# Cross products by chunk halves, layer norm on VectorE alone, and a new order of all engines in a gated delta rule kernel

## Chip, core and metric

One core of one Trainium2 chip runs the whole program. The metric is the device time in microseconds (us) of one execution. Of the kernel before there are three timed runs, and one more under the profiler.

## What is computed

One transformer block on x of shape (4 sequences, 1024 tokens, 256), in float32. A vector c gives six modulation vectors per sequence; layer norm with scale and shift feeds a gated delta rule with 16 heads of 64, and a mixture of 8 experts (2 of them per token) follows. What matters here is the delta rule:

```python
q = silu(causal_conv(x @ Wq.T)); k = ...; v = ...      # 4 taps each
k = k / norm(k)
alpha = sigmoid(h @ Wa.T + ba); beta = sigmoid(h @ Wb.T + bb)
def step(S, xs):                                        # 1024 tokens, 16 heads, 4 sequences
    upd = vt - at * (S @ kt)
    S = clip(at * S + bt * outer(upd, kt), -5, 5)
    return S, S @ qt
y = scan(step) ; out = (y * silu(h @ Wg.T + bg)) @ Wo.T
```

## The kernel before, in words

**Parts.** `front` (L132) loads x, normalises it, forms the modulation, the transposed input `hT` and the decay factors. `delta_fast` (L457) holds the instruction streams of all five engines for the delta rule, with those of `front` woven in. `attn_out` and `moe` follow after a barrier; they are untouched. A slow path (`project`, `scan`) runs only if a bound on the state was exceeded.

**Turns.** The 16 heads and 4 sequences are worked off in 16 turns (`TURNS`): turn u has the head pair u // 2 and the sequence pair u % 2. A turn is 16 chunks (`NCW`) of 64 tokens, and a chunk is made of two blocks of 32 tokens. Within a chunk the delta rule needs the inverse of a unit triangular 64 x 64 matrix. GpSimd inverts the 32 x 32 diagonal blocks by substitution (`solve`, L952 and L957, 31 steps, for all chunks, heads and sequences at once). The lower left block comes from two more products on TensorE, 32 x 32 each:

- `cross_first(u, k)` (L1547, matmul L1556) multiplies the off-diagonal block by one inverse; `keep_cross_first` (ACT, L768, L771) copies the result from PSUM to SBUF.
- `cross_second(u, k)` (L1560, matmul L1566) multiplies by the other inverse; `keep_cross` (ACT, L774, L778) copies it, negated, into `XTz`, beside the diagonal blocks that `keep_x` (ACT, L760, L765) wrote there.

The argument k is the head of the pair. One call goes through its 16 chunks and, inside, the 2 sequences b2. Operands and results lie in 32-row quadrants of the partitions, given by `quad(b2, s)`; the rows of the result also depend on the head (`cross_at`): head 0 writes quadrant (b2, s), head 1 quadrant (b2, 1 - s). So one call writes two of the four quadrants, and its 32 matmuls alternate between them. Each float32 matmul of the program stands in the trace twice.

**A software pipeline written out by hand.** The loop `for it in range(1, TURNS + 2)` stands once for each engine. In iteration `it`, turn tc = it - 1 runs its chain of chunks, turn u = it is prepared (q and v projections, solve, cross products), turn un = it + 1 gets its k projection, and turn tb = it - 2 has its bound checked. Each engine works strictly in the order in which the code issues. Inside, `c` counts the chunks of the chain. One link of the chain is `seed_u` and `state_into_u` (PE), `keep_u` (ACT, L733), `state_sum` (PE, L1616), `state` (DVE, L1055). All other work is set between the links.

**Around the end of an iteration** the order before is: PE `cross_first(u,0)`, `state_sum(13)`, `cross_first(u,1)`, `seed_u(14)`, `state_into_u(14)`, `state_sum(14)`, `cross_second(u,0)`, `seed_u(15)`, `cross_second(u,1)`, `z_turned(tb,1)` (L1544), `state_into_u(15)`, `w_product(u,0)` (L1582), `seed_u(u,0)`, `y_of_u(tc,6)` (L1644), `kk(un,0)`, `kk(un,1)` (L1463), `proj_q(un,0,0)`. ACT: `keep_x`, `keep_cross`, `keep_u(15)`, `silu_k(un)` (L699), `keep_w` (L794), `join` (L751), `keep_u(0)`. DVE: `tap_k` (L1027), `decay` (L1102), `largest_k` (L1143), `bound_scan`, `bound_max`, `solve_matrix(un)` (L1114), `update_max`, `scale_v` (L1174), `turn_matrix` (L1122), `norms`, `scalars`, `state(0)`. `kk(un,0)` writes the PSUM banks that `w_product(u,0)` used and waits for `keep_w(u,0)`; `proj_q(un,0,0)` waits for `solve_matrix(un,0)`.

**The start.** In `front`, DVE takes the moments of all four sequences and normalises sequences 0 and 2 (L297), GpSimd sequences 1 and 3 (`normalise_pool`, L344). ACT makes each sequence's root (`root`, L232) between its other work; DVE inverts it (L292). PE turns the rows (`turned`, L375). The modulation matrix `wm` comes in one transfer of 1.5 MB before sequence 1, and all its columns' products are waited for (`s_v` 4) before rows 512 to 1023 are turned. Then follow the first turn's k path, `solve(0)`, and the decay factors, which pass through HBM: `turn_gammas` (L339), eight stores, `gamma_rows(0)`, `decayed_q(0)` (L1154).

## Time and profile before

| | us |
|---|---|
| median of three runs | 1978.79 (1976.9 to 1979.03) |
| the profiled execution | 1984.33 |
| its span, first to last instruction | 1982.8 |
| start, up to the first `keep_u` of turn 0 | 151.5 |
| from there to the first `keep_u` of turn 15, 15 intervals | 1088.8 |
| last turn's chain and the end of the delta rule | about 80 |
| gate, output projection and experts | about 663 |

Busy shares of the span: PE 85%, weight loads 60%, DVE 70%, ACT 45%, POOL 56%. An interval between two turns is 70.3 to 74.5 us, 72.6 in the mean. A turn is counted from its first `keep_u`, which is easy to find: it is the first L733 on ACT behind a `join` (L751). In the timeline a row is one run of equal instructions of one engine; what stands in square brackets is the idle time before it and what ended that.

### The profile page before, as it was taken

The numbers are of one execution on the slowest core, as the hardware profiler recorded it, in microseconds if no ns is written. First come the engines' busy times: TensorE is split into PE (matmuls) and PEld (weight loads), VectorE is DVE, ScalarE is ACT, GpSimd is POOL, SyncE is SP. The second block draws the span as 40 slices with busy tenths as digits, with TensorE's granted clock in tenths as the row PEclk, the third lists the DMA queues.
The fourth block names the chain that finished last, engine by engine and source line by source line (L and its number), as shares of the span: only waits on it lengthen the run. The fifth ranks groups of instructions, "written<-read, shape, count | busy, mean of one in ns | idle before, by whom it ended". The sixth has DMA issues, their size and how long they took to land. (4 is left out here: it accounts for less than half of the span.)

```text
span 1982.8 us, 59488 instructions
## 1 busy us (share of the span) xinstructions
PE 1689.7 (85%) x24736; PEld 1185.0 (60%) x24736; DVE 1388.9 (70%) x1870; ACT 886.7 (45%) x1770; POOL 1118.4 (56%) x1379
## 2 busy tenths in 40 slices
PE   6759889999998999999998988846998749999994
PEld 3335566565665666666566556635887746666552
DVE  5667788888898888888888886447777474433331
ACT  4645545555655545555555554313435232222221
POOL 3557567568668757757767756017435014555553
PEclk9879889999889989999998987867999869999997
DMA  4121222222222212222221210237232154444442
GB/s 163 26 71 33 64 56 65 64 56 66 64 56 66 66 53 66 64 62 70 70 71 47 74 46 24 65 114 259 104 134 90 64 215 87 86 86 82 85 84 40
DMA packets 89063, 156.53 MB, mean 79 GB/s; under 512 B 15692, under 2 KB 54100, under 8 KB 87580
## 3 DMA queue, kind: packets, MB, share of 16 engines
q1 hardware_dynamic: 72892, 124.76, 20.7%
q0 software_dynamic: 15904, 27.93, 7.5%
q8 instruction: 202, 3.31, 0.7%
q14 instruction: 65, 0.53, 0.1%
HBM read 112.53 MB, written 40.12 MB: 77 GB/s over the span
## 5 line engine op out<-in xcount | busy, mean ns | idle before, releaser
L1379 PE MATMUL d_ps<-hT,turn_shared 128*128 128x512 f32 x768 | 415.1, 650 | 24.1 <-DVE d_Vp L1174 11.3
L957 POOL TENSOR_TENSOR turn_shared<-turn_shared,d_tmp 128x31 f32<-128x31 f32 (+15 forms) x496 | 288.7, 582 | 38.9
L952 POOL TENSOR_TENSOR d_tmp<-turn_shared 128x31 f32<-128x31 f32 (+15 forms) x496 | 282.8, 570 | 38.9
L1027 DVE SCALAR_TENSOR_TENSOR turn_shared<-d_ps,d_cw,turn_shared 128x1021 f32<-128x1021 f32 (+2 forms) x192 | 245.0, 1278 | 23.5 <-ACT turn_shared L684 19.6
L1379 PEld LDWEIGHTS d_ps<-hT,turn_shared 128*128 128x128 f32 x768 | 129.1, 197 | 114.3 <-issue 84.9
L2532 POOL DMA_INDIRECT out<-m_yo,m_slot_i x71 | 112.6, 1586 | 135.4 <-DVE m_yo L2632 100.2
L2511 ACT ACTIVATE m_hm<-m_ps,m_b_tile 128x128 f32<-128x128 f32 x284 | 80.9, 368 | 230.7 <-PE m_ps L2680 230.6
L733 ACT ACTIVATE d_U<-d_ps 128x128 f32<-128x128 f32 x256 | 70.3, 274 | 247.5 <-PE d_ps L1605 243.9
L2670 PE MATMUL m_ps<-m_w,m_xs 128*128 x284 | 139.3, 613 | 11.6 <-issue 10.1
L744 ACT ACTIVATE d_S<-d_S,gamma_chunk 128x64 f32<-128x64 f32 x448 | 129.6, 339 | 36.0 <-DVE d_S L1055 35.6
L2524 POOL DMA_INDIRECT m_xt<-rows_scratch,m_slot_i x71 | 70.3, 991 | 127.3 <-DVE m_slot_i L2609 95.7
L1055 DVE TENSOR_TENSOR d_S<-d_S,d_ps 128x128 f32<-128x128 f32 x224 | 62.7, 280 | 112.2 <-PE d_ps L1616 99.8
L122 PE MATMUL o_po<-wo_split,y_high 128*128 128x256 f32 x512 | 102.0, 302 | 42.0 <-DVE y_low L115 42.0
L2691 PE MATMUL m_ps<-m_w,m_hm 128*128 x568 | 134.4, 380 | 0.0
L1027 DVE SCALAR_TENSOR_TENSOR d_v_made<-d_ps,d_cw,d_v_made 128x1023 f32<-128x1023 f32 (+2 forms) x96 | 122.6, 1277 | 11.9 <-ACT d_v_made L684 10.8
L2275 POOL TENSOR_TENSOR y<-y,g_sb 128x512 f32<-128x512 f32 x48 | 78.8, 1676 | 91.9 <-ACT g_sb L2259 91.9
L1634 PE MATMUL d_ps<-d_S,d_qg 64*64 64x64 f32 x1920 | 122.6, 231 | 4.3 <-DVE d_yT L1061 2.5
L1634 PEld LDWEIGHTS d_ps<-d_S,d_qg 64*64 64x64 f32 x1920 | 88.8, 135 | 55.7 <-issue 41.7
L122 PEld LDWEIGHTS o_po<-wo_split,y_high 128*128 128x128 f32 x512 | 87.2, 209 | 44.5 <-issue 29.1
L2632 DVE SCALAR_TENSOR_TENSOR m_yo<-m_biased,m_slot_w,m_xt 128x256 f32<-128x256 f32 x71 | 34.4, 485 | 109.1 <-DMA out<-m_yo,m_slot_i 108.2
L2691 PEld LDWEIGHTS m_ps<-m_w,m_hm 128*128 128x128 f32 x568 | 102.4, 190 | 11.3 <-issue 0.4
L684 ACT ACTIVATE turn_shared<-d_ps,d_cw 128x1024 f32<-128x1024 f32 x64 | 77.1, 1204 | 60.3 <-PE d_ps L1379 26.9
(248 smaller groups left out, 3795.9 us busy)
## 6 DMA issues: line engine op xcount, KB each, us to landing
turn_shared<-steps_scratch SPq DMA_DIRECT2D x64, 256.0 KB, 4.0
d_qg<-gamma_scratch SPq DMA_DIRECT2D x64, 256.0 KB, 4.6
y_scratch<-d_yT SPq DMA_DIRECT2D x256, 64.0 KB, 2.0
d_arow<-ab_scratch SPq DMA_DIRECT2D x128, 128.0 KB, 3.0
y<-y_scratch SPq DMA_DIRECT2D x8, 2048.0 KB, 8.4
m_w<-w_in SPq DMA_DIRECT2D x16, 512.0 KB, 10.3
turn_shared<-x_by_half_in SPq DMA_DIRECT2D x8, 512.0 KB, 6.6
rows_scratch<-gates SPq DMA_DIRECT2D x4, 1024.0 KB, 12.5
```

Source lines behind the costliest of these rows:

```text
L122: ins = nc.tensor.matmul(dst, lhs(a).bitcast(F32R), rhs(b).bitcast(F32R), start=first and n == 0, stop=last and n == 2)
L744: last = nc.scalar.activation(S[:, (c + 1) % SLOTS, b2, :], S[:, c % SLOTS, b2, :], ACT.Identity, scale=gC[:, b2, tc * NCW + c:tc * NCW + ...
L952: nc.gpsimd.tensor_tensor(tv, Tq[:, s + 1:, s].rearrange("p (r a) -> p r a", a=1).broadcast_to([P, left, known]), X[:, s, 0:known].rearran ...
L957: nc.gpsimd.tensor_tensor(X[:, s + 1:, 0:known], X[:, s + 1:, 0:known], tv, ALU.subtract).then_inc(s_sub, 1)
L1027: nc.vector.scalar_tensor_tensor(out=dst[:, j + 1:], in0=src[:, 0:T - 1 - j], scalar=cw[:, u // BP % 2, n, 2 - j:3 - j], in1=dst[:, j + 1: ...
L1379: return nc.tensor.matmul(dst[:, g, :], w[:, m % 2, n, dc, :], hT[:, dc, at:at + G], start=(dc == 0), stop=(dc == DC - 1))
L1634: last = nc.tensor.matmul(y_ps(c, h, b2), qg[rows64(h), tc % 2, b2, here(c)], S[rows64(h), c % SLOTS, b2, :].rearrange("p (j v) -> p j v", ...
L2275: nc.gpsimd.tensor_tensor(y[:, g % 2, m, :], y[:, g % 2, m, :], gate_kept[g][:, m, :] if g < EARLY else g_sb[:, i % 4, :], ALU.mult).then_ ...
L2511: last = nc.scalar.activation(hm[:, j % 2, f * P:(f + 1) * P], ps[:, 2, f * P:(f + 1) * P], ACT.Gelu, bias=b1_t[:, f, j:j + 1])
L2532: nc.gpsimd.indirect_dma_start(out, bass.IndirectOffsetOnAxis(ap=slot_i[:, j:j + 1], axis=0), yo[:, j % YRING, :], None, compute_op=ALU.ad ...
L2670: last = nc.tensor.matmul(ps[:, j % 2, :], xs[:, j % 2, dc * P:(dc + 1) * P], w1_s[:, bass.ds(e, 1), dc, :].rearrange("p a f -> p (a f)"), ...
L2691: last = nc.tensor.matmul(dst, hm[:, j % 2, f * P:(f + 1) * P], w2_s[:, bass.ds(e, 1), f, :].rearrange("p a d -> p (a d)"), start=f == 0, ...
```

## The change

- `cross_first(u, hf)` and `cross_second(u, hf)` are parted by the half of the chunks instead of by the head. Inside, the loops run over chunk, head, sequence, so that four matmuls in a row write the four quadrants. The copies are no longer parted: `keep_cross_first(u)` waits for both halves and then makes its four copies, and `keep_cross(u)` likewise. Their semaphores count one per turn instead of two.
- All four sequences are normalised on DVE; `normalise_pool` goes. The clearing of `a0` moves from GpSimd to DVE.
- The columns of the modulation matrix for the first layer norm (512 of 1536) are loaded ahead; the others follow behind sequence 2, with a semaphore of their own. The products go to other PSUM banks, and the second half of the modulation is waited for before the first projection instead of before `turned(1)`.
- The order of all engines is new, at the start and in the loop. The parts of it that lie around the seam of two iterations are below. On POOL the first step of the bound of turn tb goes ahead of the last two `decay_k`. On SP `alpha_rows(tb, 1)` goes ahead of `store_y(tc, 0)`.

```diff
-            def cross_first(u, k):
+            def cross_first(u, hf):
...
-                for n in range(NCW):
-                    for b2 in range(2):
-                        last = nc.tensor.matmul(cross_at(b2, k * NCW + n, 1), TTx[quad(b2, 0), k * NCW + n, :],
-                                                Xn[quad(b2, 0), k * NCW + n, :], start=True, stop=True)
+                for n in range(hf * HC, (hf + 1) * HC):
+                    for k in range(2):
+                        for b2 in range(2):
+                            last = nc.tensor.matmul(cross_at(b2, k * NCW + n, 1), TTx[quad(b2, 0), k * NCW + n, :],
+                                                    Xn[quad(b2, 0), k * NCW + n, :], start=True, stop=True)
                 last.then_inc(s_p1, 1)
...
-            def keep_cross_first(u, k):
-                act.wait_ge(s_p1, 2 * u + k + 1)
-                for b2 in range(2):
-                    last = nc.scalar.activation(P1[quad(b2, 1), heads_of(k), :], cross_half(b2, k, 1), ACT.Identity)
+            def keep_cross_first(u):
+                act.wait_ge(s_p1, 2 * u + 2)
+                for k in range(2):
+                    for b2 in range(2):
+                        last = nc.scalar.activation(P1[quad(b2, 1), heads_of(k), :], cross_half(b2, k, 1), ACT.Identity)
                 last.then_inc(s_pe, 1)
```

The same is done to `cross_second` and `keep_cross`. The start:

```diff
-            sp.dma_start(wm[:], wmod).then_inc(s_wm, 16)
+            sp.dma_start(wm[:, :, 0:2 * D], wmod[:, :, 0:2 * D]).then_inc(s_wm, 16)
...
             rows_in(2)
+            sp.dma_start(wm[:, :, 2 * D:], wmod[:, :, 2 * D:]).then_inc(s_wr, 16)
             rows_in(3)
...
-        if g == 1:
-            pe.wait_ge(s_v, 4)
...
+            f.clear_steps(dve)
             f.moments(dve, 0)
...
             f.invert(dve, 1)
+            f.normalise(dve, 1)
+            f.moments(dve, 2)
             f.modulation(dve, 1)
-            f.moments(dve, 2)
+            f.invert(dve, 2)
             f.moments(dve, 3)
-            f.invert(dve, 2)
             f.normalise(dve, 2)
+            tap_k(0, 0, 0)
             f.invert(dve, 3)
-            tap_k(0, 0, 0)
             tap_k(0, 0, 1)
+            f.normalise(dve, 3)
...
+            f.turn_betas(dve, 0)
             turn_matrix(0)
+            norms(0)
+            scalars(0)
             tap_q(0, 0, 0)
...
             decayed_q(0)
-            largest_k(0)
+            tap_k(1, 0, 0)
+            tap_k(1, 0, 1)
             scale_v(0, 0)
+            tap_k(1, 0, 2)
             decay(1, 0)
             rows_of_x(0)
             turn_x(0)
```

The seam of two iterations after the change, each engine in its order (u is the turn prepared, tc the one in its chain, un the next):

```
PE   c13 state_into_u(13) y_of_state(tc,6,1) state_sum(13) y_of_u(tc,6) seed_u(14)
     c14 state_into_u(14) proj_k(un,1,2) proj_k(un,1,3) cross_first(u,0) cross_first(u,1) state_sum(14)
         cross_second(u,0) cross_second(u,1) z_turned(tb,1) y_of_state(tc,7,0) w_product(u,0) seed_u(15)
         y_of_state(tc,7,1)
     c15 state_into_u(15) kk(un,0) kk(un,1)
     c0  seed_u(u,0) proj_q(un,0,0) v_turned(u,1) proj_q(un,0,1) proj_q(un,0,2) state_sum(0) w_product(u,1) ...
ACT  c14 keep_u(14) first_k(un,1) keep_cross_first(u) keep_x(u) keep_cross(u) silu_k(un,0) silu_k(un,1) keep_w(u,0)
     c15 keep_u(15)
     c0  join(un) keep_u(0) carry_state(1) keep_w(u,1)
DVE  c13 state(13) rows_of_x(u) turn_x(u) tap_k(un,1,0) tap_k(un,1,1)
     c14 state(14) tap_k(un,1,2) largest_k(u) decay(un,1) bound_scan bound_max solve_matrix(un,0)
         solve_matrix(un,1) update_max scale_v(u,1) turn_matrix(un)
     c0  state(0) norms(un) scalars(un) turn_y
```

`proj_q(un,0,0)` before stood ahead of the seam's end, now behind `seed_u(u,0)`; `proj_v(u,1,2)` goes from the second half of chunk 4 to between `state_into_u(4)` and `state_sum(4)`, where `y_of_u(tc,1)` stood.

## Rows read from the trace of the kernel before

**Rows 1.** The page: busy time by engine, and PE's granted clock over 40 slices.
```profile
PE 1689.7 (85%) x24736; PEld 1185.0 (60%) x24736; DVE 1388.9 (70%) x1870; ACT 886.7 (45%) x1770; POOL 1118.4 (56%) x1379
...
PEclk9879889999889989999998987867999869999997
```
**Rows 2.** Busy us (instructions) by stage: PE, weight loads, DVE, ACT, POOL, clock, DMA.
```profile
0.00:151.50 151.50, 100.71 (x1089) 57.27 (x1090) 89.07 (x151) 80.83 (x89) 71.18 (x91) 0.86 0.28 88
...
sum 1088.80, PE 991.98 PEld 674.02 DVE 912.83 ACT 588.42 POOL 754.67; mean PE 66.13 PEld 44.93 DVE 60.86 ACT 39.23 POOL 50.31
```
**Rows 3.** Timeline of PE at a seam: start, us, what, count, [idle before <- ended by].
```profile
606.32 0.34 PE L1616 MATMUL d_ps<-d_U,gate_second 64*64 64x64 f32 x8 [1.47 <-ACT d_U L733]
...
638.97 1.20 PE L1556 MATMUL d_ps<-turn_shared 32*32 32x32 f32 x64
...
643.98 1.20 PE L1566 MATMUL d_ps<-turn_shared 32*32 32x32 f32 x64 [0.87 <-ACT turn_shared L771]
...
645.49 1.81 PE L1566 MATMUL d_ps<-turn_shared 32*32 32x32 f32 x64
647.23 1.97 PE L1544 MATMUL d_ps<-ident,d_Z 128*128 128x128 f32 x8
...
649.39 1.93 PE L1582 MATMUL d_ps<-d_XTz,d_k_by_gamma 64*64 64x64 f32 x64
...
652.91 2.27 PE L1463 MATMUL d_ps<-turn_shared 64*64 64x64 f32 x128 [0.30 <-ACT d_WT L794]
```
**Rows 4.** The same view: like groups at full clock, and groups on two or four tiles.
```profile
600.90 0.34 PE L1605 MATMUL d_ps<-d_S,d_WT 64*64 64x64 f32 x8
...
603.65 0.45 PE L1634 MATMUL d_ps<-d_S,d_qg 64*64 64x64 f32 x8
...
620.72 1.09 PE L1544 MATMUL d_ps<-ident,d_Z 128*128 128x128 f32 x8
...
659.47 1.16 PE L1582 MATMUL d_ps<-d_XTz,d_k_by_gamma 64*64 64x64 f32 x64
```
**Rows 5.** Timeline of ACT at the same seam.
```profile
643.95 2.19 ACT L765 ACTIVATE d_XTz<-turn_shared 128x1024 f32<-128x1024 f32 x2
646.23 2.40 ACT L778 ACTIVATE d_XTz<-d_ps 32x512 f32<-32x512 f32 x4
649.68 0.28 ACT L733 ACTIVATE d_U<-d_ps 128x128 f32<-128x128 f32 x1 [1.05 <-PE d_ps L1605]
649.86 1.99 ACT L699 ACTIVATE turn_shared<-turn_shared 128x1024 f32<-128x1024 f32 x2
651.75 1.01 ACT L794 ACTIVATE d_WT<-d_ps 128x1024 f32<-128x1024 f32 x1
```
**Rows 6.** Timeline of DVE at the same seam: first `tap_k`, then `solve_matrix`.
```profile
640.72 2.59 DVE L1027 SCALAR_TENSOR_TENSOR turn_shared<-d_ps,d_cw,turn_shared 128x1023 f32<-128x1023 f32 x2
...
654.13 2.48 DVE L1114 TENSOR_TENSOR turn_shared<-d_ps,turn_shared 128x512 f32<-128x512 f32 x4 [0.81 <-PE d_ps L1463]
```
**Rows 7.** Busy us by stage, as rows 2: the stretch at half clock.
```profile
645.70:652.50 6.80, 6.80 (x168) 6.32 (x160) 6.57 (x7) 5.61 (x9) 3.34 (x4) 0.50 0.31 82
```
**Rows 8.** Timelines of the start, several engines.
```profile
10.53 2.67 DVE L297 TENSOR_SCALAR gate_second<-gate_second,mv,rstd 128x256 f32<-128x256 f32 x8
...
44.28 0.20 DVE L292 RECIPROCAL rstd<-sd 128x8 f32<-128x8 f32 x1 [12.34 <-ACT sd L232]
...
44.59 11.72 POOL L344 TENSOR_SCALAR turn_shared<-turn_shared,mv,rstd 128x256 f32<-128x256 f32 x8 [16.32 <-DVE rstd L292]
...
76.46 1.90 POOL L941 TENSOR_TENSOR turn_shared<-turn_shared,d_tmp 128x1024 f32<-128x1024 f32 x1 [3.78 <-DVE d_tmp L1137]
...
116.67 3.68 POOL L986 TENSOR_TENSOR d_k_by_gamma<-gate_second,gamma_tok 128x2048 f32<-128x2048 f32 x1
...
116.89 5.61 DVE L1154 TENSOR_TENSOR d_qg<-d_qg,turn_shared 128x2048 f32<-128x2048 f32 x1 [11.98 <-DMA d_qg<-gamma_scratch]
...
127.94 2.02 DVE L1186 STREAM_TRANSPOSE turn_shared<-turn_shared 128x1024 f32<-128x1024 f32 x1
```

420 lines of the change are left out of this document (212 added, 208 removed).

## Prediction

> **What bounds the kernel now.** I read the page first. PE is busy 85% of the span and its clock is rarely below nine tenths, but DVE has 70% too, so the shares alone don't name the bound [rows 1]. The stages do. The start takes 151.5 us with PE at 100.7 and DVE at 89.1 busy: waits bound it. The 15 intervals between turns take 1088.8 us, 72.6 each, of which PE is busy 66.1 and DVE 60.9 [rows 2]: PE is the bound there, with 6.5 us of idle time in each, and DVE is close behind. The remaining 740 us (the last chain, gate, output, experts) are hardly touched by the change.
>
> Then the seam of two iterations, in the timelines. I count from the start of `cross_first(u,0)` at 638.97. PE starts `cross_second` at +5.0, after a wait of 0.87 for the copies [rows 3]. ACT runs without a pause through `keep_x` and `keep_cross`, which ends at +9.7; it then waits 1.05 for `keep_u(15)`, and `silu_k` and `keep_w` follow, to +13.8 [rows 5]. `kk(un)` starts at +13.9 [rows 3]. DVE, which began its `tap_k` at +1.75, has waited 0.81 when `solve_matrix` starts at +15.2; so it was free at +14.35 [rows 6]. Three engines are nearly level at this place, and ACT's row of copies is what ends last.
>
> In the same place PE's clock falls. From 645.7 to 652.5 the granted clock is 0.50, the lower level of 1.2 GHz [rows 7]. What went before are the cross products with PE's wait for their copies. There the second `cross_second` takes 1.81 instead of 1.20, `z_turned` 1.97 instead of 1.09, `w_product` 1.93 instead of 1.16 [rows 3, 4]: with `kk` and the short groups I put 3 to 4 us of each turn down to it. Every seam has such a stretch.
>
> **The change, part by part: the seam.** *Four quadrants.* In the new order four matmuls in a row go to four different parts of the array, before to two. The trace has the like: 8 matmuls of `state_into_u` over four places take 0.34, 8 of `y_of_state` over two take 0.45 [rows 4], so four places save 0.11 on 8 matmuls with 64 columns. A cross call has 64 with 32 columns: 0.11 x 8 / 2 = 0.45 of its 1.20. Four calls: 1.8 us of PE a turn, at full clock. The bounds are 0 (something else than the places limits the rate; the shortest rows above can't exclude it) and 2.4, half of the 4.8 us. I take 1.8 since the rows on both sides differ in the places alone.
>
> The Trainium skill, "TensorE: Matmul & The Clock Gate", section Part 1, says that matmuls never start less than about 25 ns apart, however few columns they have. By it the calls couldn't get shorter. Here 64 recorded matmuls take 1.20 us, 19 ns each [rows 3], so trace and page differ already, and I go by the trace.
>
> *Copies in one piece.* `keep_cross_first` now waits for both calls. PE: two calls of 0.75 to +1.5, `state_sum(14)` 0.34 beside. ACT: four copies, as those of `keep_cross` 2.40 together [rows 5], to +4.05. `cross_second` starts at +4.1, 0.9 earlier than before, although PE now stands idle for 2.2 us where it waited 0.87 and a little. What is queued behind this wait on PE is `cross_second`, `z_turned`, `w_product`; nothing of the chain of tc waits but chunk 15.
>
> *ACT then.* `keep_x` 2.19 to +6.25, `keep_cross` 2.40 to +8.65, `silu_k` 1.99 to +10.65, `keep_w` 1.01 to +11.7 [rows 5]. The 1.05 for `keep_u(15)` is gone, which now stands behind. `kk(un,0)` can start at +11.8 instead of +13.9.
>
> *What is late next.* DVE. Its `tap_k` starts when `first_k(un,1)` is done, as before, and its work to the end of `bound_max` is the same; `largest_k` and `decay` only change places. It is free at about +14.2. So of the 2.1 us only 0.95 arrive: `solve_matrix` at +14.2 instead of +15.2. PE, which has `z_turned`, a little of y, `w_product`, `seed_u(15)` and `kk` to do, idles 2.2 + 1.6 + 0.9 + 1.3 = 6 us up to there, where it idled 2.0. That idle time costs nothing more than the 0.95 gained; and it takes up the half clock: up to +14.2 a slow `cross_second` or `z_turned` fills idle time instead of pushing what follows. On the other hand a longer idle stretch is what went before the lower clock, so I expect the clock to fall in each seam as now, for as long or a little longer.
>
> *Behind the seam* `state(0)` no longer stands behind `norms` and `scalars`, which gives `seed_u(1)` slack but PE had other work there. At chunk 4 PE waited 1.47 for `keep_u(4)`, which stands behind the sigmoid-linear units of q on ACT [rows 3]; now a projection of about 1.0 covers it instead of a `y_of_u` of 0.7: 0.4 gained. `keep_k(u,0)` now stands behind `keep_u(5)`, and `kq(u,0)` waits for it: 0.3 lost.
>
> Sum for one interval: work of PE -1.8, half clock -3 of its 3 to 4 (hidden in idle time), idle in the seam +4, chunks 4 and 5 -0.1, together **-0.8 us**, near the 0.95 that DVE's side gives by itself. For 15 intervals -12. Bounds: -2.2 (the order also removes a third of the 6.5 us of idle time in the rest), +2.4 (below).
>
> POOL: its wait for `largest_k` and for `turn_matrix` leaves it 22 of 72.6 us idle (mean busy 50.3 [rows 2]); moving the bound's step ahead costs nothing with that cover. The two moves on SP are of transfers with a whole turn of time.
>
> **The start.** DVE waits 12.34 us for the root of sequence 3, which stands behind a projection's copy on ACT, and then GpSimd takes 11.72 for a normalisation that takes DVE 2.67 [rows 8]. Both go. DVE's additions are two normalisations (5.3) and the clearing of `a0`, which lies ahead of the first rows' arrival. Following the new order through with the durations of the rows, the two `silu_k(0)` end 10 us earlier. `scalars(0)` now stands directly behind `turn_matrix(0)`, where GpSimd waited 3.78 for it; so `solve(0)` starts at about 63 instead of 76.5 and, unchanged in length (40.2, from 76.46 to 116.67 [rows 8]), ends at 103.5. Before, the cross products had to wait further: DVE stood 11.98 us until the decay rows had come through HBM, at 116.89, and rows of X were turned only at 127.94 [rows 8]. The decay factors now come about 20 us earlier, since `mins`, `logs` and `sums` stand ahead of most v work: rows at about 95. Behind them DVE has 5.6 + 3 taps of 1.3 + 1.2 + 2.3 = 13, so X is turned at 108, 20 us earlier. From there to the first `keep_u` were 23.5 us; `join(1)` no longer comes after a `kk` that waited for `keep_w`: 21.5. Together **-22**. Bounds: -13 (only the gain of `solve` arrives) and -30 (the decay rows come when `solve` ends, and all of `silu_k(1)` is hidden).
>
> The earlier part of the modulation matrix is hidden either way: rows 512 to 1023 are turned 7 us earlier, but DVE's moments of the other sequences are later than that.
>
> **Sum.** Against the profiled execution: 1984.3 - 22 - 12 = 1950.3. That execution was 5.5 above the median of the runs, so in their terms 1978.8 - 34 = **1945 us**.
>
> **The rivals.**
> - *Other side: the seam costs more than it gives.* The copies in one piece make PE idle for 2.2 us at a stretch and leave it on short groups until `kk`. If the half clock then lasts 10 us and past +14.2, it strikes `kk`, `proj_q` and `v_turned`, which are on the path: `kk` alone goes from 2.1 to 3.5, three projections from 1 to 2 each. That is about +3.2 on -0.8: +2.4 an interval, 36 in all, and 1978.8 - 22 + 36 = 1993. The place is the seam, and it decides from +1.5 an interval, where the 22 us of the start are used up. For it: the stretch of rows 7 already follows such a wait. The same page, same section, has the rule that too little activity halves the clock; the trace agrees (0.50 behind the wait). Against: DVE's slack. 12%.
> - *Larger gain:* the new order also removes idle time in chunks 1 to 13; -2.2 an interval, 1978.8 - 22 - 33 = 1924. For it: 4 us of idle time lie there. Against: DVE would have 62 busy of 70. 20%.
> - *Start only:* the four places don't help, or DVE's end is what counts: 0 to +0.7 an interval, 1957 to 1967. 17%.
> - *Start given back:* another wait of the start, such as the step rows for `decay(1,·)`, takes over: -5 instead of -22, 1962. 6%.
>
> **How the numbers follow.** The forecast has 45%, with a range of its own of 1930 to 1960. The whole range is 1915 to 1980: it leaves out the dear end of the first rival and the far end of the second. About 0.2%, 4 us, is what a measurement of this kernel can tell from no change. Faster: 45 + 20 + 17 + most of 6, less the tails, 86%; same 4%; slower 10%.
>
> **What would show it.** Start: first `keep_u` near 129; DVE's idle before L292 under 3 us; `solve(0)` from 63. Seam: L1556 and L1566 in runs of about 0.75 at full clock; `cross_second` 4.1 behind `cross_first`; PE idle over 2 us before it <- ACT L771; L1114 no longer waiting for L1463, PE waiting for L1114 instead. Interval 71 to 72.5, DVE busy 62 in it. I am wrong if the start's decay rows come after 105, if L1556 keeps 1.20, or if the half clock reaches past `kk`.

## The result, and the profile after

The changed kernel takes 1907.72 us, the median of four runs (1898.99 to 1910.79); the kernel before, run beside it, 1978.91. The ratio is 0.9635, with a 95% interval of 0.9602 to 0.9667. That is 71 us where 34 were forecast, and 7 us below the low end of the range. The profiled execution took 1907.53 us, 76.8 less than that of the kernel before. The two traces part the 76.8 like this:

| | before, us | after, us | difference | predicted |
|---|---|---|---|---|
| start, to the first `keep_u` | 151.5 | 124.1 | -27.4 | -22 |
| 15 intervals | 1088.8 | 1049.6 | -39.2 | -12 |
| one interval, mean | 72.59 | 69.97 | -2.62 | -0.8 |
| last turn, to the end of the delta rule | 86.0 | 76.5 | -9.5 | 0 |
| gate, output, experts | 656.5 | 655.8 | -0.7 | 0 |

The line between the last two parts is the end of the delta rule in both traces; the "about 80" and "about 663" given ahead of the prediction were rough. The untouched last part took 655 to 662 us in the traces of all runs, so single traces carry some 6 us of scatter there.

The page of the changed kernel, busy time and PE's granted clock over 40 slices, for [rows 1]; behind it the start and the 15 intervals by stage, for [rows 2] (columns as there):

```profile
PE 1634.2 (86%) x24736; PEld 1146.1 (60%) x24736; DVE 1389.9 (73%) x1887; ACT 895.8 (47%) x1768; POOL 1125.9 (59%) x1362
...
PEclk9989988998998988998998996959999679999997
```
```profile
0.00:124.10 124.10, 89.28 (x1087) 51.69 (x1088) 95.62 (x167) 77.40 (x87) 48.39 (x74) 0.92 0.36 107
...
sum 1049.60, PE 955.30 PEld 643.72 DVE 907.46 ACT 599.88 POOL 784.02; mean PE 63.69 PEld 42.91 DVE 60.50 ACT 39.99 POOL 52.27
```

PE's work fell by 2.4 us an interval and its idle time, 6.5 before, is 6.3. So PE is still the busiest engine of the loop, and the shorter time did not come with the idle time that I had charged. In the start DVE is now the busiest engine.

The seam after, PE's timeline, for [rows 3]; +0 is 599.10:

```profile
599.10 1.31 PE L1570 MATMUL d_ps<-turn_shared 32*32 32x32 f32 x128
...
602.93 1.74 PE L1581 MATMUL d_ps<-turn_shared 32*32 32x32 f32 x128 [2.25 <-ACT turn_shared L770]
604.63 1.95 PE L1557 MATMUL d_ps<-ident,d_Z 128*128 128x128 f32 x8
...
607.68 1.98 PE L1599 MATMUL d_ps<-d_XTz,d_k_by_gamma 64*64 64x64 f32 x64 [0.48 <-issue]
...
610.89 3.52 PE L1471 MATMUL d_ps<-turn_shared 64*64 64x64 f32 x128 [0.16 <-ACT d_WT L794]
```

The same seam on ACT, for [rows 5]: `keep_cross`, `silu_k`, `keep_w`, and only then `keep_u(15)`:

```profile
605.19 2.39 ACT L778 ACTIVATE d_XTz<-d_ps 32x512 f32<-32x512 f32 x4
607.61 2.01 ACT L697 ACTIVATE turn_shared<-turn_shared 128x1024 f32<-128x1024 f32 x2
609.72 1.02 ACT L794 ACTIVATE d_WT<-d_ps 128x1024 f32<-128x1024 f32 x1
610.77 0.28 ACT L731 ACTIVATE d_U<-d_ps 128x128 f32<-128x128 f32 x1
```

And on DVE, the two calls of `solve_matrix`, for [rows 6]; the first has no wait, the second a short one:

```profile
612.93 1.29 DVE L1111 TENSOR_TENSOR turn_shared<-d_ps,turn_shared 128x512 f32<-128x512 f32 x2
614.47 1.29 DVE L1111 TENSOR_TENSOR turn_shared<-d_ps,turn_shared 128x512 f32<-128x512 f32 x2 [0.24 <-PE d_ps L1471]
```

The places of the seam come out close to the forecast, within 0.4 us: both calls of `cross_first` in one run, `cross_second` at +3.8 (forecast +4.1) behind 2.25 of idle time, `keep_cross` done at +8.5 (+8.65), `kk` at +11.8 (+11.8), `solve_matrix` at +13.8 (+14.2). PE's clock is at 0.50, its lower level, from +4.3 to +14.5 here, in the stage view:

```profile
603.40:613.60 10.20, 9.44 (x286) 8.56 (x278) 10.05 (x10) 7.36 (x10) 6.85 (x5) 0.50 0.26 67
```

From `cross_first` to the next `keep_u(0)` the turns 2 to 14 took 20.99 us in the mean before and 19.20 after; the rest of an interval 51.68 and 51.24. But this mark has moved: `cross_first` now stands behind `state_into_u(14)`, one link later in the chain, so the split is not of like with like. The chain's own marks don't move. Over the same turns `keep_u(0)` to `keep_u(13)` went from 49.33 to 47.37 us and `keep_u(13)` to the next `keep_u(0)` from 23.34 to 23.07: of 2.2 us an interval, 2.0 lie behind the seam. The link from `keep_u(4)` to `keep_u(5)` alone went from 4.9 to 3.1 and the one from `keep_u(9)` from 4.0 to 2.7, while others grew; the work of PE between the links was moved as well. The first and the last interval, whose neighbours are the start and the last turn, gave 4.7 and 5.5.

The start after, for [rows 8]: `solve(0)` on GpSimd, then on DVE `decayed_q(0)`, which no longer waits, and `rows_of_x(0)`:

```profile
59.35 1.90 POOL L937 TENSOR_TENSOR turn_shared<-turn_shared,d_tmp 128x1024 f32<-128x1024 f32 x1 [0.74 <-DVE d_tmp L1134]
...
92.91 2.46 DVE L1151 TENSOR_TENSOR d_qg<-d_qg,turn_shared 128x2048 f32<-128x2048 f32 x1
...
103.76 2.04 DVE L1183 STREAM_TRANSPOSE turn_shared<-turn_shared 128x1024 f32<-128x1024 f32 x1
```

### The profile page after: what moved, and what is told of

It reads as the page before. It is cut to its first block and busy times, and to the rows that moved or that the text cites. A ratio compares the mean times of both kernels' runs of the same rounds, so it can differ in the third digit from the quotient of the medians.

```text
span 1906.0 us, 59470 instructions
## 1 busy us (share of the span) xinstructions
PE 1634.2 (86%) x24736; PEld 1146.1 (60%) x24736; DVE 1389.9 (73%) x1887; ACT 895.8 (47%) x1768; POOL 1125.9 (59%) x1362
## 5 line engine op out<-in xcount | busy, mean ns | idle before, releaser
L1386 PE MATMUL d_ps<-hT,turn_shared 128*128 128x512 f32 x768 | 404.4, 635 | 8.9 <-DVE d_Vp L1171 4.7
L948 POOL TENSOR_TENSOR d_tmp<-turn_shared 128x31 f32<-128x31 f32 (+15 forms) x496 | 292.1, 589 | 38.9
L953 POOL TENSOR_TENSOR turn_shared<-turn_shared,d_tmp 128x31 f32<-128x31 f32 (+15 forms) x496 | 284.0, 573 | 38.9
L1024 DVE SCALAR_TENSOR_TENSOR turn_shared<-d_ps,d_cw,turn_shared 128x1023 f32<-128x1023 f32 (+2 forms) x192 | 245.3, 1278 | 15.9 <-ACT turn_shared L682 13.4
L1651 PE MATMUL d_ps<-d_S,d_qg 64*64 64x64 f32 x1920 | 134.8, 243 | 1.1
L1651 PEld LDWEIGHTS d_ps<-d_S,d_qg 64*64 64x64 f32 x1920 | 98.7, 145 | 26.5 <-issue 21.5
```

The costliest lines, as they stand in the source:

```text
L948: nc.gpsimd.tensor_tensor(tv, Tq[:, s + 1:, s].rearrange("p (r a) -> p r a", a=1).broadcast_to([P, left, known]), X[:, s, 0:known].rearran ...
L953: nc.gpsimd.tensor_tensor(X[:, s + 1:, 0:known], X[:, s + 1:, 0:known], tv, ALU.subtract).then_inc(s_sub, 1)
L1024: nc.vector.scalar_tensor_tensor(out=dst[:, j + 1:], in0=src[:, 0:T - 1 - j], scalar=cw[:, u // BP % 2, n, 2 - j:3 - j], in1=dst[:, j + 1: ...
L1386: return nc.tensor.matmul(dst[:, g, :], w[:, m % 2, n, dc, :], hT[:, dc, at:at + G], start=(dc == 0), stop=(dc == DC - 1))
L1651: last = nc.tensor.matmul(y_ps(c, h, b2), qg[rows64(h), tc % 2, b2, here(c)], S[rows64(h), c % SLOTS, b2, :].rearrange("p (j v) -> p j v", ...
```

## The experiments

My first theory was that the shorter cross products and the earlier `kk` carry the loop's gain. The rival was that the new order elsewhere does. All ratios are to the kernel before, run beside each on the same chip, since that kernel's own median moved between 1977 and 1984 from one set of runs to the next; 0.1% is 2 us. "After" is 0.9635. A difference between two variants of the changed kernel carries both their intervals, 8 to 13 us to each side: it is given in brackets there.

| kernel | ratio, 95% interval | from its neighbour, us |
|---|---|---|
| after, cross products over two parts of the array | 0.9701 (0.9672 to 0.9729) | +13 from after (5 to 22) |
| after, `keep_u(15)` first on ACT | 0.9855 (0.9830 to 0.9880) | +44 (35 to 52) |
| after, spare matmuls | 0.9648 (0.9625 to 0.9671) | +3, not told apart |
| after, 1.23 us more on DVE in 8 turns | 0.9653 (0.9627 to 0.9679) | +4, not told apart |
| after, `largest_k` late | 0.9691 (0.9657 to 0.9726) | +11 (2 to 20) |
| after, both of spare and late | 0.9753 (0.9716 to 0.9790) | +23 (14 to 33) |
| after, `proj_v` back in chunk 4 | 0.9752 (0.9714 to 0.9791) | +23 (13 to 33) |
| after, cross products one link earlier | 0.9668 (0.9635 to 0.9701) | +7, not told apart |
| after, `carry_state` late | 0.9736 (0.9691 to 0.9781) | +20 (9 to 31) |
| after, `norms` ahead of `state(0)` | 0.9741 (0.9708 to 0.9775) | +21 (12 to 30) |
| after, last turn's order of before | 0.9639 (0.9583 to 0.9696) | +1, not told apart |
| after, normalisation on GpSimd | 0.9709 (0.9651 to 0.9767) | +15 (1 to 28) |
| before, four parts | 0.9933 (0.9907 to 0.9958) | -13 from before |
| before, `keep_u(15)` last on ACT | 1.0057 (1.0038 to 1.0076) | +11 |
| before, these two | 1.0032 (1.0014 to 1.0049) | +6 |
| before, `keep_u(15)` last and `kk` early | 0.9960 (0.9936 to 0.9983) | -8 |
| before, all three | 0.9933 (0.9902 to 0.9964) | -13 |
| before, the start alone | 0.9911 (0.9876 to 0.9946) | -18 |

### The parts of the array, in both orders

```diff
-                for n in range(hf * HC, (hf + 1) * HC):
-                    for k in range(2):
+                for k in range(2):
+                    for n in range(hf * HC, (hf + 1) * HC):
                         for b2 in range(2):
```

> The changed kernel, but inside each of its two cross calls the loop over the head pairs stands outside again, so that matmuls in a row alternate between two parts of the array and not four; instruction count, waits, copies and the order of all engines stay. Theory A (the four parts carry most of what an interval gained): a call takes 1.2 us again instead of 0.65, PE has 2.2 us more work a turn, the copies start 1.1 later, kk starts at +12.9 instead of +11.8 behind cross_first, and the interval grows by 0.9 to 2.2 us, 14 to 33 in all: 1922 to 1941 us. Theory B (the new order of the engines carries it, DVE's end at the seam hides the cross products): under 0.4 an interval, so 1914 at most.

The kernel before got the change's loops and joined copies, as shown in the diff ahead of the prediction, with its own order kept:

> The kernel before with this part of the change alone: the cross products run by halves of the chunks over both head pairs, with the copies of a half pair joined behind both calls; start, order of all engines and everything else as before. Theory A (four parts of the array): cross calls of 0.65 us, PE 2 us less busy a turn, the row of copies ends about 1 us earlier, interval -1.0 to -1.8, sum 15 to 27: 1952 to 1964 us. Theory B (order carries it; here ACT's wait for keep_u(15) and the queue order remain): -0.3 or less an interval, 1974 to 1980 us.

13 us come back in the one and 13 go in the other. In the trace of the first, two calls in one run take 1.93 us instead of 1.31, the interval is 70.7 instead of 70.0, and the seam 20.0 instead of 19.2. In the trace of the second, where each call stands alone, one takes 0.75 instead of the 1.20 of [rows 3]. PE's timelines of both:

```profile
605.76 1.93 PE L1570 MATMUL d_ps<-turn_shared 32*32 32x32 f32 x128
```
```profile
630.82 0.75 PE L1554 MATMUL d_ps<-turn_shared 32*32 32x32 f32 x64
```
So the four parts are worth 0.7 us an interval in either order, a little under the low end of theory A, and they are about a quarter of what the loop gained, not most of it.

In the kernel before the seam got 0.9 shorter, but the rest 0.3 longer, and the place is chunk 4. PE's timeline and the stage view of that run:

```profile
454.51 0.46 PE L1615 MATMUL d_ps<-d_U,gate_second 64*64 64x64 f32 x8 [1.47 <-ACT d_U L733]
454.90 3.51 PE L1376 MATMUL d_ps<-hT,turn_shared 128*128 128x512 f32 x4
```
```profile
454.90:458.30 3.40, 3.40 (x8) 1.45 (x6) 3.27 (x3) 0.41 (x1) 3.24 (x3) 0.54 0.02 5
```

It is the wait of [rows 3], 1.47 us for `keep_u(4)`, and behind it the clock falls for 3.4 us; two projections take 3.51 instead of 1.98, and the link from `keep_u(4)` to `keep_u(5)` 6.1 to 6.2 instead of 4.5. Of the 12 turns from 2 to 13 this befell 3 in the kernel before, 7 with the four parts, and none in the changed kernel, where the link takes 3.0 to 3.1 in every turn. These are single traces, and that the four parts bring the falls about is not shown: in the later run that has them together with `keep_u(15)` last, it befell 3 turns of 12.

### `keep_u(15)` and `keep_w` on ACT

```diff
-                    if new_k and c == 14:
+                    if new_k and c == 15:
                         silu_k(un, 0)
                         silu_k(un, 1)
-                    if prep and c == 14:
+                    if prep and c == 15:
                         keep_w(u, 0)
```

> The changed kernel with one move undone: on ACT silu_k(un,.) and keep_w(u,0) stand behind keep_u(15) again, as in the kernel before. My prediction's step: 1 us of waiting comes back on ACT, kk starts at +12.9 to +13.3, DVE is ready at +13.8, so only the second kk can delay it: +0.3 to +1.0 an interval, 1912 to 1923 us. Rival (what counts is only when the copies of the cross products are done; keep_u(15) is ready by then, because w_product is earlier too): no change, 1906 to 1910 us.

Neither: it costs 44 us (41 between the two medians), and the interval is 72.5, as before the change. The seam at 613.89 of that run, on PE, ACT and DVE:

```profile
628.78 3.69 PE L1471 MATMUL d_ps<-turn_shared 64*64 64x64 f32 x128 [3.26 <-ACT d_WT L794]
...
632.83 1.87 PE L1386 MATMUL d_ps<-hT,turn_shared 128*128 128x512 f32 x2
```
```profile
625.55 0.28 ACT L731 ACTIVATE d_U<-d_ps 128x128 f32<-128x128 f32 x1 [3.19 <-PE d_ps L1622]
```
```profile
630.82 1.29 DVE L1111 TENSOR_TENSOR turn_shared<-d_ps,turn_shared 128x512 f32<-128x512 f32 x2 [3.17 <-PE d_ps L1471]
```
```profile
617.30:634.40 17.10, 13.12 (x370) 11.40 (x371) 13.45 (x15) 8.54 (x12) 7.90 (x5) 0.50 0.44 122
```

The wait is 3.19 and not the 1.05 of [rows 5], because the new order puts `state_into_u(15)` behind `w_product`. Everything behind is late by it: `kk` waits 3.26, DVE 3.17. And with PE's longer pause the clock is at its lower level for 17.1 us, past `kk` and over the projections (1.87 for one instead of 1.12). So the half clock of my first rival does reach `kk` and the projections here, though behind another wait than the one it named. The price is 2.5 us an interval in the trace, where the rival had 3.2. How much of it is the clock's is not shown: the wait of 3.2 by itself covers it. The change itself avoids it by putting `keep_w` first.

Does the move help by itself, in the kernel before?

```diff
-                    if prep and c == 0:
-                        silu_k(u, 0)
-                        silu_k(u, 1)
-                    if chain and c == 0:
-                        keep_w(tc, 0)
...
                         keep_cross(u, 1)
+                    if new_k and c == 14:
+                        silu_k(un, 0)
+                        silu_k(un, 1)
+                    if prep and c == 14:
+                        keep_w(u, 0)
```

> The kernel before with one move alone: on ACT silu_k(un,.) and keep_w(u,0) stand ahead of keep_u(15). Undone in the changed kernel, this move cost 41 us, although the wait that it removes is 1.05 us a turn in the kernel before. Theory A (the price depends on the order around it: here keep_u(15) is ready at +10.7, there only at +12): ACT's row ends 1.05 earlier, DVE can take at most its 0.81 of waiting back, so -0.3 to -0.9 an interval, 1966 to 1977 us. Theory B (the move has the same worth in every order): -2.5 an interval, about 1940 us.

> The kernel before with the four parts of the array and that move on ACT together. By itself the first gave 0.7 an interval, 12 us. Theory A (each shortens the same row of copies; DVE then has nothing left to wait for, so the second gives less than by itself): -0.8 to -1.4 an interval from before, 1960 to 1970 us. Theory B (they help each other, as in the new order, where undoing either costs much): -2.5 or more, 1943 us or less.

It harms, by 11 us, and with the four parts the sum is still 6 above the kernel before; all theories were wrong. PE's and ACT's timelines at 647.42 (`w_product`) of the first of these runs show two new waits:

```profile
647.42 1.93 PE L1585 MATMUL d_ps<-d_XTz,d_k_by_gamma 64*64 64x64 f32 x64
650.71 0.70 PE L1599 MATMUL d_ps<-d_Vp,d_XTz 64*64 64x64 f32 x8 [1.36 <-issue]
```
```profile
649.42 1.02 ACT L794 ACTIVATE d_WT<-d_ps 128x1024 f32<-128x1024 f32 x1 [0.72 <-PE d_ps L1585]
650.34 0.27 ACT L733 ACTIVATE d_U<-d_ps 128x128 f32<-128x128 f32 x1
```

ACT now reaches `keep_w` before `w_product`, whose result it copies, has ended, and waits 0.72 for it. `keep_u(15)` stands behind that and starts 2.9 us behind the start of `w_product`, where it was 0.3, and `seed_u(u,0)`, which by the code waits for `keep_u(15)`, stands on PE for 1.36 us with `kk` queued behind it. The row "issue" names no releaser; that it is this wait is read from the code and from the 0.1 us between the end of `keep_u(15)` (650.61) and the start of PE (650.71). The next pair moves `kk` ahead of `seed_u`:

```diff
                         w_product(u, 0)
-                        seed_u(u, 0)
                     if chain and c == 15:
                         y_of_u(tc, 6)
                     if new_k and c == 15:
                         kk(un, 0)
                         kk(un, 1)
+                    if prep and c == 15:
+                        seed_u(u, 0)
+                    if new_k and c == 15:
                         proj_q(un, 0, 0)
```

> The kernel before with two moves: on ACT silu_k(un,.) and keep_w(u,0) ahead of keep_u(15), and on PE kk(un,0) and kk(un,1) ahead of seed_u(u,0). The first alone made the kernel 11 us slower: the trace of that run shows PE standing 1.36 us ahead of seed_u(u,0), which by the code waits for keep_u(15), and kk behind it. Theory A (that new wait was the whole loss): the 11 us are given back and kk starts 0.5 earlier than in the kernel before, -0.2 to -0.6 an interval, 1969 to 1976 us. Theory B (keep_u(15) late costs elsewhere too, at the chain's own end): still 1980 or more.

> The kernel before with those two moves and the four parts of the array: all that my prediction named of the seam, with nothing of the new order elsewhere. The changed kernel's interval is 2.6 us shorter. Theory A (these three are the seam's gain): -1.6 to -2.4 an interval, 1943 to 1955 us. Theory B (the rest of the new order is needed too: y_of_state and y_of_u moved out of the seam, state_into_u(15) behind w_product, the projections placed ahead of the cross products): -0.6 to -1.4 an interval, 1957 to 1970 us.

The first is theory A: the 11 us come back and 8 more go. The second is theory B, at its weak end: -13 us, where four parts and pair by themselves give 13 and 8. Its seam is 20.0, 1.0 shorter; chunk 4's fall of the clock, now in 8 of 12 turns, takes most of that back: the 15 intervals of this trace are together only 3.1 us shorter than before, and 3.9 come from the start. So all that I had named of the seam gives 13 us in the old order. Most of the loop's gain had to be elsewhere.

### The places that I had priced at nothing

Each of these undoes one place in the changed kernel. `proj_v(u,1,2)`, which the change put ahead of `state_sum(4)`, goes behind it:

```diff
-                    if prep and c == 4:
-                        proj_v(u, 1, 2)
...
                         state_sum(tc, c)
...
                     if prep and c == 4:
+                        proj_v(u, 1, 2)
                         k_turned(u, 0)
```

> The changed kernel with proj_v(u,1,2) back in the second half of chunk 4, behind state_sum(4), where the kernel before has it. PE stood 1.47 us there before, 0.49 after the change. Theory A (my prediction's step: only this wait): it comes back as about 1.4, +0.4 an interval, 6 us: 1911 to 1916. Theory B (the longer wait also lets the clock fall behind it, as a second stretch at half clock in chunk 4 of two variants of the kernel before shows): +0.8 to +1.3 an interval, 1920 to 1928 us. Theory C: a later wait takes it up, no change.

+23 us, theory B. The link from `keep_u(4)` to `keep_u(5)` takes 4.0 instead of 3.0 to 3.1 in seven of the turns 2 to 13, and 5.6 in five, where the clock's mean over it is 0.69 or 0.70. 15 x 0.95 for the wait and 5 x 1.6 for the falls are 22 in this link. Not all of it arrives: the trace's 15 intervals are 11.7 us longer, since other links got shorter (the first one by 0.4, the seam by 0.5). That is 0.8 an interval, the low end of theory B.

`norms(u)` and `scalars(u)` go ahead of `state(0)` on DVE:

```diff
+                    if prep and c == 0:
+                        norms(u)
+                        scalars(u)
                     if chain and c < NCW - 1:
                         state(tc, c)
-                    if prep and c == 0:
-                        norms(u)
-                        scalars(u)
```

> The changed kernel with norms(u) and scalars(u) on DVE ahead of state(0) again. By my prediction PE had other work there and this move was worth nothing: 1906 to 1911 us. Rival: state(0) comes 1.5 to 2 us later, with it seed_u(1) and the whole chain of the turn; PE's other work does not cover it and the interval is 0.5 to 1.5 longer, 1915 to 1930 us. In between: POOL's solve starts as much earlier as state(0) comes later, and cross_first with it, which gives part back.

`carry_state` goes back to its old places on ACT, for most chunks one chunk later, all else as in the changed kernel:

```diff
                     if chain and c == 0:
-                        carry_state(tc, 1)
                         keep_w(tc, 1)
+                    if chain and c == 1:
+                        carry_state(tc, 1)
...
-                    if chain and c == 2:
-                        carry_state(tc, 3)
...
+                    if chain and c == 3:
+                        carry_state(tc, 3)
```

> The changed kernel with carry_state on ACT where the kernel before has it: carry_state(tc,c), which state(c) on DVE waits for, stands in chunk c behind keep_u(c) for most c, not in chunk c - 1. Theory A (the last turn, where the copies of gate, 0.68 us, stand between keep_u and carry_state, got its 9.5 us from this): the last turn takes 82 to 87 us instead of 76.5, an interval 0 to 0.5 more, 1913 to 1925 us. Theory B (the last turn got shorter by its order of y_of_state and y_of_u on PE): last turn under 79 and 1905 to 1911 us.

PE's waits over ten turns, in us, times and the longest one. First the kernel before (`state_sum` for `keep_u`), then the changed kernel, then `norms` first, then `carry_state` late, then `proj_v` back:

```profile
PE d_ps L1616 <- ACT d_U L733: 22.9, 40, 1.5
```
```profile
PE d_ps L1581 <- ACT turn_shared L770: 22.4, 10, 2.2
PE d_ps L1633 <- ACT d_U L731: 9.2, 28, 0.5
```
```profile
PE d_ps L1613 <- DVE d_S L1049: 12.5, 10, 1.3
```
```profile
PE d_ps L1631 <- ACT d_U L731: 19.6, 40, 1.0
```
```profile
PE d_ps L1633 <- ACT d_U L731: 20.3, 30, 1.5
```

So the wait of `state_sum` for `keep_u` went from 2.3 to 0.9 us a turn by the change. With `norms` first `seed_u(1)` waits 1.25 us a turn for `state(0)`, and the link from `keep_u(0)` to `keep_u(1)` takes 5.9 instead of 4.4. That is the rival, +21 us (13.4 over the trace's 15 intervals), not my "worth nothing". With `carry_state` late the waits of `state_sum` for `keep_u` double, and the links that begin with `keep_u(1)`, `keep_u(3)` and `keep_u(5)` are 0.3 to 0.5 longer: +20 (17.9 over the trace's 15 intervals). The last turn stays at 77.3, so its gain isn't from there.

The cross products themselves, with their projections, one link earlier (and `first_k(un,1)` on ACT ahead of `keep_u(14)`):

```diff
                         y_of_u(tc, 6)
+                    if new_k and c == 13:
+                        proj_k(un, 1, 2)
+                        proj_k(un, 1, 3)
+                    if prep and c == 13:
+                        cross_first(u, 0)
+                        cross_first(u, 1)
                     if chain and c == 13:
                         seed_u(tc, 14)
```

> The changed kernel with proj_k(un,1,2), proj_k(un,1,3) and both calls of cross_first one link earlier: ahead of seed_u(14) instead of behind state_into_u(14), with first_k(un,1) on ACT ahead of keep_u(14), about as in the kernel before. Theory A (this place is the larger part of the loop's gain: now the four copies follow the cross products at once, there keep_u(14) and its state_into_u(14) come between): the copies start at +2.3 instead of +1.4, cross_second at +4.8 to +5.3 instead of +3.8, the seam gets 0.8 to 1.5 longer, 1918 to 1931 us. Theory B (the work merely changes sides of the mark from which I count): within 0.3 an interval, 1905 to 1913 us.

`cross_second` starts at +4.9 as theory A says, and the seam is 20.1. But the rest is 0.9 shorter: the work changes sides of my mark, and +7 us in all, where the two kernels' intervals overlap, is nearer to theory B. This place does not matter much. It does correct the split by my mark: with `cross_first` at its old place in the chain the seam is 0.9 shorter than before the change, and the rest, 50.4 instead of 51.7, is 1.3 shorter.

Not all of the new order was undone. The projections in other chunks, DVE's order in chunks 1 to 13 and GpSimd's no run gives back by themselves. On GpSimd the change also moves `gamma_k` and the first two `decay_k` one iteration forward, which the section on the change does not say; over ten turns, before and after, no wait of PE was ended by GpSimd.

The last turn, with PE's and DVE's order of before in the last two iterations. Of the edit, PE's chunks 9 to 11:

```diff
+                    state_into_u(15,9)
+                    gate(7,0)
+                    state_sum(15,9)
+                    gate(7,1)
+                    seed_u(15,10)
+                    state_into_u(15,10)
+                    gate(8,0)
+                    y_of_state(15,4,1)
+                    state_sum(15,10)
+                    gate(8,1)
+                    seed_u(15,11)
+                    y_of_u(15,4)
+                    y_of_state(15,5,0)
+                    state_into_u(15,11)
```

> The changed kernel with the order of PE and DVE in the last turn's iteration and the one behind it as in the kernel before (y_of_state, y_of_u, z_turned, turn_y, update_max at their old places); all other turns and engines unchanged. From keep_u(0) to keep_u(15) this turn takes 54.1 us in the changed kernel and 62.4 in the one before. Theory A (the order of the output products around the links, with their waits for turn_y, makes the links of 3 us into such of 4 to 5): 59 to 63 us again and the whole time 5 to 9 us longer, 1913 to 1917. Theory B (the chain gets its data earlier by ACT's new order): at most 1 us longer, 1906 to 1910 us.

The times can't tell (0.9583 to 0.9696). In the trace, from `keep_u(0)` to `keep_u(15)` the last turn takes 64.1 us, 54.1 in the changed kernel, 62.4 before. Every other variant of the changed kernel has 53.0 to 57.0 there, so theory A holds for this turn; that the whole time follows is not shown. PE has waits in it on the transposes of y and on the state, which the changed kernel doesn't have:

```profile
PE d_ps L1695 <- DVE d_yT L1058: 2.5, 2, 1.6
PE d_ps L1657 <- DVE d_S L1052: 1.8, 2, 1.3
```

They make 4.3 of the 10.0; where the rest lies was not followed up.

### What bounds the seam now

One more reduction on DVE, in the first 8 turns whose bound is scanned:

```diff
                         bound_scan(tb, 1)
+                        if tb < 8:
+                            nc.vector.tensor_reduce(more[:, tb:tb + 1], flat(z_pair(tb, 1)), AX_X, ALU.max)
                         bound_max(tb, 1)
```

> The changed kernel with one more reduction of 1.23 us on DVE right ahead of bound_max, at the seam, in 8 of the intervals (the last before them and the 7 others run without it, so both kinds stand in one trace). It writes a tile that nobody reads. My prediction took DVE to be what sets the seam. Theory A (it does): the intervals with it are 0.9 to 1.3 us longer than those without, 7 to 10 us in all: 1915 to 1918. Theory B (PE with ACT's row ahead of kk sets it, DVE's end is 0.3 us early or level by chance): the intervals with it are longer by 0.3 to 0.6 at most, 1910 to 1913 us. Theory C: something behind the seam takes it up: no difference.

The 8 intervals with it are 71.4 us in the mean and the same ones of the changed kernel 70.8. The 7 without it are 0.25 shorter than theirs, so between 0.65 and 0.9 of the 1.23 arrives, between A and B. DVE's row is nearly level with another.

The spare matmuls go ahead of `cross_second`, into banks that `w_product` fills later:

```diff
+            def spare(u, n):
+                pe.wait_ge(s_ktap[0], 3 * u + 6)
+                for i in range(n):
+                    nc.tensor.matmul(pair(AT_W[0])[:, i % 2, :], ident[:], hT[:, 0, 0:G], start=True, stop=True)
...
                     if prep and c == 14:
+                        if u + 1 < TURNS:
+                            spare(u, 2)
                         cross_second(u, 0)
```

> The changed kernel with two added matmuls of 128 x 512 a turn, whose product nobody reads, in the pause of PE between cross_first and cross_second. They take some 0.3 to 0.45 us each and fit into the pause of 2.25. Theory A (the pause lets the clock fall, and kk at half clock is on the way to the next keep_u): the time at the lower clock falls from 9.7 us a seam to under 6, kk from 3.5 to about 2.1, the seam gets 1.0 to 1.5 shorter: 1885 to 1895 us. Theory B: the clock falls nevertheless, for as long, because the short products and not the pause are what goes before it; then the time is 1905 to 1912 us. Theory C: the clock stays up, but DVE's end at +13.8 sets the seam: 1903 to 1908 us.

The two take 1.98 us together, more than I had allowed for, and fill most of the pause. The time at the lower clock fell to 4.75 us a seam, from 9.71, and nothing was gained. PE at the seam that begins at 596.66, with the releasers on ACT and DVE:

```profile
598.18 1.98 PE L1577 MATMUL d_ps<-hT,ident 128*128 128x512 f32 x4
...
608.44 1.22 PE L1471 MATMUL d_ps<-turn_shared 64*64 64x64 f32 x64 [0.16 <-ACT d_WT L794]
610.56 1.16 PE L1471 MATMUL d_ps<-turn_shared 64*64 64x64 f32 x64 [0.90 <-DVE beta_turned L1091]
```

It is theory C. `kk` starts at +11.8 whatever the clock, because ACT's row sets that, and its second half then waits for `bound_max` on DVE. Moving 2.27 us of DVE out of the way, alone and with the spare ones:

```diff
-                    if prep and c == 14:
-                        largest_k(u)
...
                         solve_matrix(un, 1)
+                    if prep and c == 14:
+                        largest_k(u)
```

> The changed kernel with largest_k(u), 2.27 us on DVE, behind solve_matrix(un,1) instead of ahead of decay(un,1). In the trace of the changed kernel solve_matrix(un,0) starts at +13.8 without a wait, right behind bound_max, while kk(un,1) runs at half clock and ends at +15.2. Theory A (DVE's row sets the seam): solve_matrix starts up to 2.2 earlier, join and keep_u up to 0.9 earlier, the interval gets 0.5 to 0.9 shorter: 1894 to 1901 us. Theory B (kk at half clock is level with DVE): solve_matrix waits for kk and at most 0.3 an interval is gained, 1903 to 1909 us; the work that now stands behind may even delay turn_matrix.

> The same move together with the two spare matmuls of 128 x 512 in PE's pause ahead of cross_second. With the spare matmuls alone kk(un,0) ran at full clock (1.22 us) but kk(un,1) then stood 0.90 us for bound_max on DVE, and the time was unchanged. Theory A (clock and DVE's row were level, so only both together help): solve_matrix starts at about +13.0 and ends by +15.2, keep_u 1.0 to 1.8 earlier, 1880 to 1893 us. Theory B (something third is level too, such as v_turned, join or the chain behind): 1900 to 1909 us.

Both lose, 11 and 23 us. DVE's timeline in the first:

```profile
615.58 2.65 DVE L1111 TENSOR_TENSOR turn_shared<-d_ps,turn_shared 128x512 f32<-128x512 f32 x4 [2.19 <-PE d_ps L1471]
618.14 2.28 DVE L1140 TENSOR_REDUCE d_kmax<-d_ktok 128x128 f32<-128x2048 f32 x1
```

All that DVE saved turned into a wait of 2.19 for `kk`, and `largest_k` then stands ahead of `scale_v` and `turn_matrix`. ACT's row, PE's `kk` and DVE's row end within 0.3 us of one another; none can be shortened alone. Why the pair lost more than the move alone is open.

### The start

The kernel before with the changed `front` and the start's order as shown ahead of the prediction, its loop and its cross products untouched:

> The kernel before with the changed front part and the start's order of the change alone; loop and cross products as before. The trace of the changed kernel has its first keep_u 27.4 us earlier, at 124.1. Theory A (that is the start's own gain and all of it arrives): first keep_u at 124 to 127, time lower by 24 to 28: 1953 to 1958 us. Theory B (3 to 5 us of the 27 belong to the cross products and to the loop's order): first keep_u at 128 to 131, 1958 to 1963 us.

The first `keep_u` comes at 127.1, theory A by the trace (-24.4); the timed gain of 18 (11 to 25) is smaller, near theory B. About 3 us of the 27 belong to the cross products and the order behind them: the kernel before with the four parts alone has its first `keep_u` at 148.0, 3.5 earlier.

```diff
-            f.normalise(dve, 1)
-            f.normalise(dve, 3)
...
+            f.normalise_pool(pool, 1)
+            f.normalise_pool(pool, 3)
```

> The changed kernel with the layer norm of sequences 1 and 3 on GpSimd again (11.72 us each in the trace of the kernel before, 2.67 on DVE). My prediction's step: for sequence 3 the rows come 9 us later to TensorE and with them the first turn's v and q work. Theory A (the step carries a good part of the 27 us of the start): first keep_u at 128 to 134 instead of 124, 1911 to 1918 us. Theory B (solve(0) and the cross products wait for sequences 0 and 1 alone, and the second sequence pair's input is needed only later): first keep_u within 1 us, 1906 to 1910 us.

+15 us, the first `keep_u` at 138.8, 14.7 later. Both theories were too small, and sequence 3 is not alone in it. GpSimd's and PE's timelines of this run:

```profile
17.71 9.65 POOL L346 TENSOR_SCALAR gate_second<-gate_second,mv,rstd 128x256 f32<-128x256 f32 x8 [17.04 <-DVE rstd L294]
41.09 10.93 POOL L346 TENSOR_SCALAR turn_shared<-turn_shared,mv,rstd 128x256 f32<-128x256 f32 x8 [13.73 <-DVE rstd L294]
...
69.25 1.90 POOL L943 TENSOR_TENSOR turn_shared<-turn_shared,d_tmp 128x1024 f32<-128x1024 f32 x1 [0.73 <-DVE d_tmp L1142]
```
```profile
27.51 1.58 PE L377 MATMUL d_ps<-ident,gate_second 128*128 128x128 f32 x8 [3.74 <-POOL gate_second L346]
...
46.06 1.07 PE L377 MATMUL d_ps<-ident,turn_shared 128*128 128x128 f32 x8 [2.15 <-POOL turn_shared L346]
...
52.16 1.07 PE L377 MATMUL d_ps<-ident,turn_shared 128*128 128x128 f32 x8 [2.34 <-POOL turn_shared L346]
...
58.65 1.57 PE L1477 MATMUL d_ps<-turn_shared 64*64 64x64 f32 x92 [1.87 <-ACT turn_shared L703]
```

Sequence 1 belongs to the first pair, and its 9.65 instead of 2.67 hold up the first turn's k path: DVE's first `tap_k` starts at 39.60 instead of 33.58, 6.0 later. Sequence 3 does not belong to it, but PE turns its rows ahead of `kk(0)` and waits 2.15 and 2.34 for them: `kk(0)` starts at 58.65 instead of 48.75, 9.9 later, and `solve(0)` at 69.25 instead of 59.35. What makes 14.7 of the 9.9 up to the first `keep_u` was not followed.

## Why the prediction was wrong, by its own steps

**The start: right, a little small.** -27.4 lies inside -13 to -30. `solve(0)` from 59.35 (forecast 63), `decayed_q` at 92.91 (95), `rows_of_x` at 103.76 (108), the first `keep_u` at 124.1 (129). The step's weights were off: I followed sequence 3's root and its 11.72. Of the first 9.9 us that normalising on GpSimd costs, 6.0 have come by the first `tap_k`, by sequence 1; the other 3.9 come where PE waits for sequence 3's rows.

**The four parts: right in size.** A call that stands alone went from 1.20 to 0.75 us, the 0.45 of the estimate. Of two calls in one run the four parts save 0.62 (1.93 to 1.31), since running them on end shortens them as well. 0.7 us an interval of it arrived.

**The seam's order: places right, two of its terms not.** Every time from +0 to `solve_matrix` came within 0.4 us. The base was one of the shortest seams of the kernel before, 19.8 us, where the mean is 21.0. Still the 0.95 was about right: with the mark at the same place of the chain the seam gave 0.9. The terms "idle in the seam +4" and "half clock -3" overlap: groups at half clock fill the pause, so PE's idle time there grew only from 3.0 to 3.8, with 9.7 us a seam at the lower clock instead of 8.5; over a whole interval the idle time fell from 6.5 to 6.3. And removing a wait of 1.05 was not a gain of 1.05 or less but part of a set: alone it cost 11 us, in the new order its absence costs 44.

**"Behind the seam": this step failed.** I gave -0.1 for all of it, and the runs show -1.3 an interval, or -2.0 by the chain's own marks. Chunk 4 alone was 23 us when undone (11.7 over its trace's intervals), since the wait of 1.47 went to 0.49 and the falls of the clock behind it, which [rows 7] had shown me only for the seam, went with it. `state(0)` ahead of `norms` "gives slack but PE had other work there": undone it costs 21. `carry_state` a chunk earlier I didn't name at all: 20. By the whole change PE's wait for `keep_u` went from 2.3 to 0.9 us a turn. They do not add up to the 39 us of the loop, nor would they with the 44 and the 13; each undone place shows the length of a wait that the others may hide or feed. How the 39 us part among them, and with the moves that no run undid, stays open.

**The tail: not looked at.** I took 0 for the last turn without reading its waits; it gave 9.5. With PE's and DVE's old order of the output's work in it, 10.0 us come back in the trace.

**Sums of the prediction that do not come out.** The four terms of an interval, -1.8, -3, +4 and -0.1, make -0.9 and not -0.8. The first rival's terms, 1.4 for `kk` and 1 for each of three projections, make 4.4, where it went on with 3.2.

**The rivals.** The larger gain, -2.2 an interval, is the one that came in the loop (-2.6), and its reason, idle time in chunks 1 to 13, is the right one in part: idle time of PE behind the seam fell from 3.1 to 2.1 us. The other side did not come; a half clock over `kk` and the projections came in the run with `keep_u(15)` first, behind another wait.

## What to carry to other kernels

Price a step at its mean over the turns, not at the one seam that was opened, and read the last turn as closely as the middle one. Split an interval at marks that the change does not move. Where an instruction of the serial chain moves past other work on its engine, follow what in the next engine's queue stands behind the receiver: the same move cost 11 us or saved 44 by what stood there. Behind a wait of 1.5 us on TensorE its clock fell in some turns and not in others, and the link was then 1.6 us longer.
